# Moving the shared expert's second half product by a unit, with other banks and GpSimd for the first weight splits

## The chip, the cores and the metric

The kernel runs on one core of a Trainium2 chip. The metric is the device time of one execution in microseconds (us). Without the change it is 989.12 us, the median of three runs (989.07 to 989.73).

## The reference, cut to what matters

Sixteen sequences of 100 tokens with 512 features go through gated cross attention on 361 context keys each, and then through a feed-forward part with eight routed experts and one shared expert:

```python
x = x + tanh(g_xattn[0]) * xattn(layernorm(x), ctx_2048, Wq, Wk, Wv)   # 32 heads of 16, RMS-normed q and k
x = x + tanh(g_ffn[0]) * ffn(layernorm(x), router_w, w_gate_up, w_down, shared_gate_up, shared_down)
# ffn: router logits -> best expert e and gate = sigmoid(logit)
#   routed = silu(g) * u @ w_down[e],  (g, u) = (h * gate) @ w_gate_up[e]
#   shared = silu(g) * u @ shared_down, (g, u) = h @ shared_gate_up
#   return routed + shared
```

## The kernel before, in words

All engines run orders written out by hand in numbered **slots**. The loop over slots (L394 for TensorE, L528 for ScalarE, L690 for VectorE, L938 for GpSimd, L1333 for the DMA queue of SyncE) goes to slot 389; each engine does in slot s what is listed for s, in order, and semaphores make it wait. Sequence b is scored in slots 24b to 24b+23 as six **units** of four slots each: z = 0, 1 is the half of the heads, t = 0, 1, 2 the tile of keys. Unit n of sequence b is written (b, n) here, n = 3z + t.

For one unit TensorE makes scores (pe_scores, L490, into banks 4 to 7), ScalarE takes exp of them (act_exp, L663), and TensorE multiplies the probabilities with the values (pe_weighted_values, L505, called PV here, into bank 1). The next unit's scores wait for this unit's exp. Behind PV of n = 2 and n = 5 ScalarE takes bank 1 (act_take_outputs, L679 or L681) and so frees it for the next PV. For b < 15 a DMA transpose (L1314), a GpSimd copy (pool_join, L911), two small VectorE operations (dve_invert, L880 and L883) and two of GpSimd (pool_finish, L919 and L921) then bring the outputs back to x_all. For b = 15, TensorE turns them (pe_turn_outputs, L517, into bank 0) and VectorE finishes (dve_finish_last, L892 to L898).

Beside the scoring of b, sequence b+1 is prepared: projections (L472), sums of squares (L837), an inverse root in ten dependent steps on VectorE (dve_rms, L847 and then L769, L771, L773, L774), scaling (dve_scale, L859), packing into a high and a low f16 part (ScalarE L656, VectorE L866) and a transposing DMA each for the three key tiles and the queries (sp_turn_pack, L1307). Scores of unit (15, 0) wait for that of the queries (qT), whose issue in turn waits until q, key tile 0 and key tile 1 are all packed. In the last sequence ScalarE's packing of key tile 2 stands ahead of the exp of (15, 0) in its order. Nothing is projected beside the scoring of sequence 15, as there is no sequence 16.

The first piece of the feed-forward part is put into this thin stretch. The first weights of the shared expert are split into high and low parts in four pieces of 128 x 512: ScalarE writes high (act_first_high, L1409, slots 347, 348, 353, 354) and VectorE low = weight - high (dve_first_low, L1415, slots 348, 349, 356, 357). Pieces 0 and 1 are gate and up for the product's half j = 0, pieces 2 and 3 for j = 1. TensorE multiplies j = 0 in slots 351 (gate, bank 3) and 355 (up, bank 2), twelve matmuls each; VectorE copies both out (dve_first_copy, L1421). The half j = 1 comes in four **quarters** of six matmuls (pe_gate_up, L1475, slots 365, 369, 373, 377) into the same banks 3 and 2. In slot 386 the gate product of the next chunk follows. Then pe_shared begins, whose line of routing transposes (L1026) goes to banks 2 and 3 in turn, the first only when VectorE has multiplied (dve_mult, L1547) both halves of iteration 0. The slots of the last sequence on TensorE, as they run: 359 scores (15, 0); 363 scores (15, 1); 364 PV 0; 365 quarter; 367 scores 2; 368 PV 1; 369 quarter; 371 scores 3; 372 PV 2; 373 quarter; 374 turn of the outputs z = 0; 375 scores 4; 376 PV 3; 377 quarter; 379 scores 5; 380 PV 4; 384 PV 5; 386 next product; 387 turn of z = 1.

turn_order and wait_turn_bank (L365 and L432) keep the users of bank 0 in order, and product_bank (L1443) gives the bank of each gate and up product.

Of the kernel before, what the change touches and what calls it, by code (L numbers as in the profile page):

```python
# [20 lines left out]
F32 = mybir.dt.float32  # L21
# [18 lines left out]
HD = 16  # L40
# [38 lines left out]
FIRST_LOW_SLOTS = (348, 349, 356, 357)  # L79
FIRST_PRODUCT_SLOTS = (351, 355)  # L80
FIRST_COPY_SLOTS = (361, 362)
SECOND_PRODUCT_SLOTS = (365, 369, 373, 377)
NEXT_PRODUCT_SLOT = 386

DOWN_SLOT = 381
# [253 lines left out]
    return 24 * (b - 2) + LEAD  # L339


LAST_OUT_SLOTS = (14, 27)


def scoring(k, s):
    return [(b, s - 24 * b) for b in range(k.B) if 0 <= s - 24 * b < 40]
# [18 lines left out]
def turn_order(k):  # L365

    order = []
    for s in range(k.first_slot, k.last_slot):
        for b, j in preparing(k, s):
            order += [("src", b)] if j == SRC_SLOTS[2] else []  # L370
        for b, i in scoring(k, s):
            order += [("out", b, z) for z in range(2) if b == k.B - 1 and i == LAST_OUT_SLOTS[z]]
        for c, o in route_offsets(s):
            order += [("route", c, i) for i, at in enumerate((*ROUTE_TURN, ROUTE_LOGITS, ROUTE_BACK, ROUTE_RANK))
                      if o == at]
    return order, {name: n for n, name in enumerate(order)}
# [52 lines left out]
    return w  # L429


def wait_turn_bank(k, w, name):  # L432
    place = k.turn_place[name]
    if place:
        kind, *at = k.turn_names[place - 1]
        if kind == "src":
            w.wait_ge(k.src_low, 4 * at[0] + 3)
        elif kind == "out":
            w.wait_ge(k.finish_v, 2 * at[1] + 2)
        else:  # L440
            wait_route_taken(k, w, *at)


def pe_turn_source(k, PE, w, b):
    w.wait_ge(k.ident32_made, 2)
    w.wait_ge(k.xn_made, b + 1)
    wait_turn_bank(k, w, ("src", b))
    bank = k.bank[0]
    for j in range(k.KD):
        turned = PE.transpose(bank[:, P * j:P * j + k.N], k.xn[:, P * j:P * j + P], k.ident32[0:k.N, 0:k.N])  # L450
    turned.then_inc(k.src_turned, 1)
# [59 lines left out]

def pe_turn_outputs(k, PE, w, b, z):
    w.wait_ge(k.outs_taken, 2 * b + z + 1)
    wait_turn_bank(k, w, ("out", b, z))
    bank = k.bank[0]
    for j in range(4):
        turned = PE.transpose(bank[0:k.N, P * j:P * j + P], last_outs(k, z)[:, j, :], k.ident32[:])  # L517
    turned.then_inc(k.last_out_turned, 1)
# [5 lines left out]
def act_attention(k):  # L524
    A, w = k.A, Waits(k.A)
    for i, g in enumerate((k.g_xattn, k.g_ffn)):
        A.dma_start(k.gates[:, i:i + 1], g.rearrange("(a n) -> a n", a=1).to_broadcast([P, 1])).then_inc(k.gates_in, 16)
    for s in range(k.first_slot, k.last_slot):  # L528
        for n in (n for n, at in enumerate(WEIGHT_SLOTS) if prep_start(0) + at == s):
            act_weight_high(k, A, w, n)  # L530
        if s == prep_start(0) + 16:
            w.wait_ge(k.constants_made, k.n_constants)
        if unit_at(k, s):
            act_exp(k, A, w, s)
        for b, j in preparing(k, s):
            for p in range(4):
                if j == SRC_SLOTS[p] + 1:
                    act_source_high(k, A, w, b, TILE[p])
        if s == prep_start(0) + 16:
            w.wait_ge(k.gates_in, 32)  # L540
            A.activation(k.gates[:], k.gates[:], ACT.Tanh).then_inc(k.gates_ready, 1)
        for b, j in preparing(k, s):
            for n in range(7):
                if j == taken_slot(n):
                    if n in VALUE_AT:
                        act_copy_values(k, A, w, b, PROJECTION_TILE[n])
                    else:
                        act_take_heads(k, A, w, b, PROJECTION_TILE[n])
            for t in range(4):
                if j == PACK_SLOTS[t] + 1:  # L550
                    act_pack_high(k, A, w, b, t)
        for b, i in scoring(k, s):
            for z in range(2):
                if i == pv_slot(k, b, 3 * z + 2) + 1:
                    act_take_outputs(k, A, w, b, z)
        if s == ROUTER_SLOT:
            w.wait_ge(k.router_in, 16)
            A.activation(k.wrT[0][:], k.w_router_raw[:], ACT.Copy).then_inc(k.router_high, 1)
        for c, o in route_offsets(s):
            for j in range(CT):  # L560
                if o == ROUTE_TURN[j] + 1:
                    act_route_high(k, A, w, c, j)
            if o == ROUTE_LOGITS + 1:
                act_route_logits(k, A, w, c)
            if o == ROUTE_BACK + 2:
                act_route_gate(k, A, w, c)
        for n in range(4):
            if s == FIRST_SLOTS[n]:
                act_first_high(k, A, w, n)
        if s == DOWN_SLOT:  # L570
            act_part_high(k, k.first, A, w, 2)
    return w
# [114 lines left out]
def dve_attention(k):  # L687
    V, w = k.V, Waits(k.V)
    V.memset(k.bank[1][:, 0:GH * k.N], 0.0).then_inc(k.outs_cleared, 1)
    for s in range(k.first_slot, k.last_slot):  # L690
# [42 lines left out]
        for c, o in route_offsets(s):  # L733
# [12 lines left out]
                dve_route_place(k, V, w, c)  # L746
            if o == ROUTE_RANK + 2:
                dve_route_slot(k, V, w, c)
        for n in range(4):
            if s == FIRST_LOW_SLOTS[n]:  # L750
                dve_first_low(k, V, w, n)
        for which in range(2):
            if s == FIRST_COPY_SLOTS[which]:
                dve_first_copy(k, V, w, which)
# [131 lines left out]
def dve_finish_last(k, V, w, b, z):  # L886

    x, _, o = finish_views(k, b, z)
    turned = k.bank[0][0:k.N, :].rearrange("n (h c) -> n h c", c=2 * HD)
    w.wait_ge(k.x1_made, 2 * b + z)  # L890
    w.wait_ge(k.last_out_turned, z + 1)
    V.reciprocal(k.inv_sum[:], turned[:, :, HD]).then_inc(k.finish_v, 1)  # L892
    w.wait_ge(k.finish_v, 2 * z + 1)
    V.tensor_tensor(o, turned[:, :, 0:HD], k.inv_sum[:].unsqueeze(2).to_broadcast([k.N, 16, HD]),
                    MULT).then_inc(k.finish_v, 1)
    w.wait_ge(k.gates_ready, 1)
    w.wait_ge(k.finish_v, 2 * z + 2)
    V.scalar_tensor_tensor(out=x, in0=o, scalar=k.gates[0:k.N, 0:1], in1=x, op0=MULT, op1=ADD).then_inc(k.x1_made, 1)  # L898
# [25 lines left out]
def pool_attention(k):  # L924
# [13 lines left out]
    for s in range(k.first_slot, k.last_slot):  # L938
        for b, i in scoring(k, s):
            for z in range(2):  # L940
                if b + 1 < k.B and i == OUT_JOIN_SLOTS[z]:
                    pool_join(k, G, w, b, z)
                if b + 1 < k.B and i == OUT_JOIN_SLOTS[z] + 3:
                    pool_finish(k, G, w, b, z)
        for c, o in route_offsets(s):
            for j in range(CT):
                if o == ROUTE_GATED[j]:
                    pool_store_gated(k, G, w, c, j)
            if o == ROUTE_RELOAD:
                pool_reload(k, G, w, c)  # L950
        if s == FIRST_LOAD_SLOT:
            w.wait_ge(k.src_low, 4 * k.B)
            w.wait_ge(k.src_turned, k.B)
            for t in k.rows[2:4]:
                G.memset(t[:], 0.0).then_inc(k.rows_cleared, 1)
    return w


# [13 lines left out]
def wait_route_bank(k, w, c, i):  # L972

    place = route_place(c, i)
    if c < EARLY:
        wait_turn_bank(k, w, ("route", c, i))
    elif place < 4:
        w.wait_ge((k.first.mult, k.first.silu)[place % 2], 2)
    else:
        c_, i_ = divmod(place - 4, 7)  # L980
        wait_route_taken(k, w, c_ + EARLY, i_)
# [427 lines left out]
    A.activation(high, src, ACT.Copy).then_inc(k.first_high if n < 2 else k.first.w_high, 1)  # L1409


def dve_first_low(k, V, w, n):
    src, high, low = first_views(k, n)
    w.wait_ge(k.first_high if n < 2 else k.first.w_high, n % 2 + 1)
    V.tensor_tensor(low, src, high.bitcast(F32), SUB).then_inc(k.first_low if n < 2 else k.first.w_low, 1)  # L1415


def dve_first_copy(k, V, w, which):
# [14 lines left out]
def dve_part_low(k, r, V, w, part):  # L1433
    u, which = divmod(part, 3)
    high, low = k.w_split[u % 3][which]
    w.wait_ge(r.w_high, part + 1)
    V.tensor_tensor(low[:], k.w_raw[part % 4][:], high[:].bitcast(F32), SUB).then_inc(r.w_low, 1)  # L1437


# [3 lines left out]
def product_bank(r, it, j, which):  # L1443


    if it >= r.it0:
        return 2 * j + which
    return (3 - which, 4 + 2 * j + which, which)[min(it, 2)]


def pe_gate_up(k, r, PE, w, it, u, j, which, xs, width, share=0, shares=1):
# [8 lines left out]
    if r.it0 and it == 0:  # L1460
        if j == 0:
            w.wait_ge((k.v_copied, k.squared)[which], (k.NMT, k.NMT + 1)[which] * k.B)
        else:
            w.wait_ge(k.first_copied, which + 1)
    elif r.it0 and it == 1:
        w.wait_ge(k.exped, 6 * k.B)
    elif it <= r.it0:
        if r.it0 and it == 2:
            w.wait_ge(k.finish_v, 4)
        w.wait_ge(taken, 2 * it + (j if it < r.it0 else 0))  # L1470
    else:
        w.wait_ge(taken, 2 * it + j - 1)
# [613 lines left out]
```

## Time and profile before

| | value |
|---|---|
| median of three runs | 989.12 us |
| the profiled execution's own time | 988.57 us |
| its span | 986.6 us |
| TensorE busy in the span | 957.0 us, 97% |
| VectorE, ScalarE, GpSimd busy | 672.4, 559.2 and 161.7 us |
| mean granted TensorE clock | 0.997 |
| TensorE waits longer than noise from 550 us on | none |

Times in the rows count from the start of the span. In the page, PE is TensorE's matmuls, PEld its weight loads, DVE VectorE, ACT ScalarE, POOL GpSimd, SPq the DMA queue of SyncE. Between the profiled execution's time and its span lie 1.97 us of start and end.

### The profile page before, as it was taken

The page shows a single profiled execution, that of the slowest core. Times are in us where ns is not written, and L with a number is a line of the kernel's source. Part 1 is how long each engine was busy: PE and PEld are TensorE (multiplying, and loading weights), DVE is VectorE, ACT ScalarE, POOL GpSimd, SP SyncE. Part 2 cuts the span into 40 slices and gives each one's busy share as a digit, 9 for nine tenths or more (in the row PEclk, how much of TensorE's full clock was granted, in tenths as well). Part 3 has the DMA queues.
Part 4 walks back from the last instruction along what each step waited for, and adds up shares of the span by engine and source line. Part 5 has one row for each costly group of instructions (what it writes and reads, how often), then busy time and mean ns, then how long its engine had stood idle before and what let it go on. Part 6 is the DMA issues. An engine that isn't in the chain of part 4 may idle for free. (4 is left out here: it accounts for less than half of the span.)

```text
span 986.6 us, 25132 instructions
## 1 busy us (share of the span) xinstructions
PE 957.0 (97%) x10589; PEld 784.5 (80%) x10589; DVE 672.4 (68%) x1647; ACT 559.2 (57%) x851; POOL 161.7 (16%) x208
## 2 busy tenths in 40 slices
PE   5899999999999999999889999999999999999997
PEld 4677777777777777777777999999988988999886
DVE  6878886877658678687747534443477777777774
ACT  5576767777666777766752221222256666666663
POOL 2001111110112210112233300000110232012111
PEclk9999999999999999999999999999999999999999
DMA  7544344654337554346543401010377886787762
GB/s 263 142 92 84 78 91 105 122 90 88 80 73 169 110 100 83 71 91 150 128 101 107 114 22 43 22 43 21 123 239 224 243 244 215 220 244 240 224 197 69
DMA packets 176425, 127.38 MB, mean 129 GB/s; under 512 B 117246, under 2 KB 155134, under 8 KB 176308
## 3 DMA queue, kind: packets, MB, share of 16 engines
q1 hardware_dynamic: 166884, 105.98, 43.0%
q0 software_dynamic: 6544, 16.46, 5.4%
q10 hardware_dynamic: 2880, 3.29, 1.0%
q8 instruction: 85, 1.39, 0.6%
q14 instruction: 32, 0.26, 0.1%
HBM read 85.52 MB, written 13.56 MB: 100 GB/s over the span
## 5 line engine op out<-in xcount | busy, mean ns | idle before, releaser
L472 PE MATMUL bank<-arena_f32r 128*128 128x512 f32 (+2 forms) x1344 | 334.8, 400 | 11.4 <-DVE arena_f32r L823 10.1
L472 PEld LDWEIGHTS bank<-arena_f32r 128*128 128x128 f32 (+2 forms) x1344 | 234.8, 180 | 78.5 <-DVE arena_f32r L780 10.6
L663 ACT ACTIVATE probs<-score_banks 128x1600 f32<-128x1600 f32 x96 | 144.6, 1506 | 58.1 <-PE score_banks L490 58.0
L1536 ACT ACTIVATE hT_hi<-arena_f 128x224 fp32r<-128x224 f32 (+2 forms) x96 | 42.3, 441 | 116.7 <-DVE arena_f L1547 111.3
L1475 PE MATMUL bank<-xnT,arena_f32r 128*128 128x224 f32 (+1 forms) x720 | 103.2, 295 | 0.0
L1475 PEld LDWEIGHTS bank<-xnT,arena_f32r 128*128 128x128 f32 x720 | 97.7, 191 | 1.9 <-issue 0.8
L505 PEld LDWEIGHTS bank<-probs,values 128*17 128x17 f32 (+1 forms) x3072 | 62.7, 98 | 37.4 <-issue 22.3
L505 PE MATMUL bank<-probs,values 128*17 128x100 f32 (+1 forms) x3072 | 85.1, 252 | 3.2 <-ACT probs L663 2.5
L1547 DVE TENSOR_TENSOR arena_f<-bank,arena_f 128x224 f32<-128x224 f32 (+2 forms) x93 | 41.2, 443 | 65.6 <-PE bank L1475 65.1
L1437 DVE TENSOR_TENSOR arena_f32r<-arena_f,arena_f32r 128x1024 fp32r<-128x1024 f32 x43 | 52.7, 1226 | 19.2 <-ACT arena_f32r L1430 18.1
L911 POOL COPY heads_out<-outs 100x544 uint16<-100x544 uint16 x30 | 25.3, 843 | 203.6 <-DMA outs<-outT 202.8
L837 DVE TENSOR_REDUCE sumsq<-arena_f 128x32 f32<-128x512 f32 (+1 forms) x64 | 43.8, 685 | 21.5 <-ACT arena_f L625 21.4
L1562 PE MATMUL score_banks<-arena_f32r,hT_hi 128*128 128x512 f32 (+2 forms) x184 | 58.0, 396 | 0.0
L490 PE MATMUL score_banks<-qT,kT 32*128 32x100 f16 x3072 | 51.7, 205 | 5.5 <-ACT probs L663 3.0
L1493 PE MATMUL bank<-xnT,arena_f32r 128*128 128x448 f32 x168 | 55.8, 377 | 0.0
L1562 PE MATMUL score_banks<-wdown_lo,hT_hi 128*112 128x512 f32 (+2 forms) x140 | 55.1, 394 | 0.0
L1562 PE MATMUL score_banks<-wdown_hi,hT_hi 128*112 128x512 f32 (+2 forms) x140 | 55.1, 393 | 0.0
L490 PEld LDWEIGHTS score_banks<-qT,kT 32*128 32x128 f16 x3072 | 37.4, 93 | 20.9 <-issue 15.3
L1526 ACT ACTIVATE arena_f<-bank 128x384 f32<-128x384 f32 (+1 forms) x29 | 14.6, 505 | 64.9 <-PE bank L1475 64.7
L823 DVE TENSOR_TENSOR arena_f32r<-arena_f,arena_f32r 128x512 fp32r<-128x512 f32 (+1 forms) x48 | 31.9, 665 | 27.8 <-ACT arena_f32r L608 27.5
L1430 ACT ACTIVATE arena_f32r<-arena_f 128x1024 fp32r<-128x1024 f32 x43 | 45.1, 1048 | 8.4 <-DVE x_all L1720 8.4
L1720 DVE SCALAR_TENSOR_TENSOR x_all<-score_banks,gates,x_all 128x512 f32<-128x512 f32 (+1 forms) x52 | 38.6, 748 | 14.1 <-PE score_banks L1562 13.8
(275 smaller groups left out, 1850.8 us busy)
## 6 DMA issues: line engine op xcount, KB each, us to landing
arena_f<-L_ffn_w_gate_up SPq DMA_DIRECT2D x48, 512.0 KB
arena_f<-L_ffn_w_down SPq DMA_DIRECT2D x24, 512.0 KB
arena_f<-ctx SPq DMA_DIRECT2D x15, 722.0 KB, 4.2
w_raw<-L_ffn_w_gate_up SPq DMA_DIRECT2D x16, 512.0 KB
w_raw<-L_ffn_w_down SPq DMA_DIRECT2D x8, 512.0 KB
x_rows<-x_all SPq DMA_DIRECT2D x4, 800.0 KB
x_all<-x_rows POOLq DMA_DIRECT2D x4, 768.0 KB, 5.7
arena_f<-L_ffn_shared_gate_up SPq DMA_DIRECT2D x6, 512.0 KB
```

The lines of the kernel that those rows point to most:

```text
L472: product = PE.matmul(bank[0:rows, :], k.srcT[PLACE[t] % 2][a][:, j, 0:rows], weight, start=(m == 0), stop=(m == 11))
L490: product = PE.matmul(k.score_banks[:, j, k.N * r:k.N * r + k.N], k.kT[b % 2][rows, block, P * t:P * t + P], k.qT[b % 2][rows, part, block ...
L505: product = PE.matmul(k.bank[1][HW * j:HW * j + HD + 1, k.N * r:k.N * r + k.N], k.values[b % 2][0:m, t, 16 * z + GH * r + j, :], k.probs[n ...
L663: A.activation(k.probs[n % 2][:], k.score_banks[:, :, 0:GH * k.N].rearrange("p j (r n) -> p j r n", r=GH), ACT.Exp, scale=float(HD) ** -0. ...
L837: V.tensor_reduce(k.sumsq[b % 2][0:rows, t, :], k.square[0:rows, :].rearrange("p (h d) -> p h d", d=HD), AX.X, ADD).then_inc(k.summed, 1)
L1430: A.activation(k.w_split[u % 3][which][0][:], k.w_raw[part % 4][:], ACT.Copy).then_inc(r.w_high, 1)
L1437: V.tensor_tensor(low[:], k.w_raw[part % 4][:], high[:].bitcast(F32), SUB).then_inc(r.w_low, 1)
L1475: made = PE.matmul(bank[:, 0:width], weight[a][:, i, :], xs[x][:, i, 0:width], start=(i == 0 and n == 0), stop=(i == k.KD - 1 and n == 2))
L1493: PE.matmul(bank[:, 0:2 * SLOTS].rearrange("p (x n) -> p x n", x=2), high[:, i, :], xs[:, :, i, 0:SLOTS], start=(i == 0), stop=False)
L1536: A.activation(k.hT[it % 2][0][:, j, 0:width], k.hidden[j][:, 0:width], ACT.Copy).then_inc(r.h_high, 1)
L1547: V.tensor_tensor(h, up[:, 0:width], h, MULT).then_inc(r.mult, 1)
L1562: made = PE.matmul(bank[0:rows, :], k.hT[it % 2][h][:, j, r0:r0 + rows], weight[a][:, j, :], start=(first and j == 0 and n == 0), stop=(la ...
```

## The change

It has four parts. The quarters move to slots 361, 366, 370 and 373, and the two gate quarters go into bank 0 instead of bank 3, waiting for bank 0's last user in place of the copy of bank 3. The low parts of the four first weight pieces are made by GpSimd, at the end of the same slots, in place of VectorE. ScalarE takes the outputs of (14, z = 1) in slot 360, behind the exp of (15, 0), instead of slot 359 ahead of it. The last sequence's outputs are turned in bank 3 instead of bank 0, and later waits on the banks are changed to suit.

```diff
-SECOND_PRODUCT_SLOTS = (365, 369, 373, 377)
+SECOND_PRODUCT_SLOTS = (361, 366, 370, 373)
...
-LAST_OUT_SLOTS = (14, 27)
+LAST_OUT_SLOTS, LAST_OUT_BANK = (14, 27), 3
...
-        for b, i in scoring(k, s):
-            order += [("out", b, z) for z in range(2) if b == k.B - 1 and i == LAST_OUT_SLOTS[z]]
...
-def wait_turn_bank(k, w, name):
-    place = k.turn_place[name]
+def wait_turn_bank(k, w, place):
...
-        elif kind == "out":
-            w.wait_ge(k.finish_v, 2 * at[1] + 2)
...
     w.wait_ge(k.outs_taken, 2 * b + z + 1)
-    wait_turn_bank(k, w, ("out", b, z))
-    bank = k.bank[0]
+    w.wait_ge(*((k.finish_v, 2) if z else (k.first_copied, 1)))
+    bank = k.bank[LAST_OUT_BANK]
...
-                if i == pv_slot(k, b, 3 * z + 2) + 1:
+                if i == pv_slot(k, b, 3 * z + 2) + (2 if (b, z) == (k.B - 2, 1) else 1):
                     act_take_outputs(k, A, w, b, z)
...
-        for n in range(4):
-            if s == FIRST_LOW_SLOTS[n]:
-                dve_first_low(k, V, w, n)
...
-    turned = k.bank[0][0:k.N, :].rearrange("n (h c) -> n h c", c=2 * HD)
+    turned = k.bank[LAST_OUT_BANK][0:k.N, :].rearrange("n (h c) -> n h c", c=2 * HD)
...
+        for n in range(4):
+            if s == FIRST_LOW_SLOTS[n]:
+                pool_first_low(k, G, w, n)
...
-        w.wait_ge((k.first.mult, k.first.silu)[place % 2], 2)
+        w.wait_ge(*((k.finish_v, 4) if place % 2 else (k.first.mult, 2)))
...
-def dve_first_low(k, V, w, n):
+def pool_first_low(k, G, w, n):
     src, high, low = first_views(k, n)
     w.wait_ge(k.first_high if n < 2 else k.first.w_high, n % 2 + 1)
-    V.tensor_tensor(low, src, high.bitcast(F32), SUB).then_inc(k.first_low if n < 2 else k.first.w_low, 1)
+    G.tensor_tensor(low, src, high.bitcast(F32), SUB).then_inc(k.first_low if n < 2 else k.first.w_low, 1)
...
     w.wait_ge(r.w_high, part + 1)
+    w.wait_ge(r.w_low, 2 if r.u0 and part == 2 else 0)
...
-    return (3 - which, 4 + 2 * j + which, which)[min(it, 2)]
+    return (0 if (j, which) == (1, 0) else 3 - which, 4 + 2 * j + which, which)[min(it, 2)]
...
+        elif which == 0:
+            wait_turn_bank(k, w, len(k.turn_names))
         else:
-            w.wait_ge(k.first_copied, which + 1)
+            w.wait_ge(k.first_copied, 2)
...
         if r.it0 and it == 2:
-            w.wait_ge(k.finish_v, 4)
+            w.wait_ge(k.outs_taken, 2 * k.B)
```

## Rows read from the trace of the kernel before

**Rows 1.** The page, busy time, and the granted clock in 40 slices

```profile
PE 957.0 (97%) x10589; PEld 784.5 (80%) x10589; DVE 672.4 (68%) x1647; ACT 559.2 (57%) x851; POOL 161.7 (16%) x208
PEclk9999999999999999999999999999999999999999
```

**Rows 2.** Timeline of TensorE's matmuls: start, duration, line, operation, count, idle before

```profile
476.39 0.33 PE L1475 MATMUL bank<-xnT,w_first_gate_lo 128*128 128x384 f32 x1
477.83 0.53 PE L490 MATMUL score_banks<-qT,kT 32*128 32x100 f16 x32 [1.11 <-ACT probs L663]
...
482.37 0.53 PE L490 MATMUL score_banks<-qT,kT 32*128 32x100 f16 x32 [0.20 <-DMA qT<-q_pack]
484.85 0.77 PE L490 MATMUL score_banks<-qT,kT 32*128 32x100 f16 x32 [1.94 <-ACT probs L663]
485.55 1.54 PE L505 MATMUL bank<-probs,values 128*17 128x100 f32 x32
487.01 1.94 PE L1475 MATMUL bank<-xnT,arena_f32r 128*128 128x384 f32 x6
...
490.16 1.34 PE L1475 MATMUL bank<-xnT,arena_f32r 128*128 128x384 f32 x6
...
493.97 0.64 PE L517 MATMUL bank<-ident,outT 128*100 128x128 f32 x4
...
499.60 0.88 PE L505 MATMUL bank<-probs,values 105*17 105x100 f32 x32 [0.80 <-ACT probs L663]
...
505.75 0.54 PE L1026 MATMUL bank<-ident,rows 100*128 100x100 f32 x4 [0.44 <-DVE arena_f L1547]
```

**Rows 3.** Busy time of each engine in stretches, with granted clock (PEclk) behind POOL

```profile
484.00:485.00 1.00, 0.15 (x15) 0.18 (x19) 0.43 (x1) 0.70 (x1) 0.40 (x1) 1.00 0.50 100
485.00:486.00 1.00, 1.00 (x44) 0.85 (x39) 0.53 (x3) 0.34 (x1) 0.40 (x1) 0.50 0.98 180
488.00:489.00 1.00, 1.00 (x17) 0.76 (x19) 0.69 (x1) 0.00 (x0) 0.47 (x1) 0.80 0.61 136
```

**Rows 4.** Timeline of ScalarE

```profile
473.19 0.65 ACT L1409 ACTIVATE w_first_up_hi<-arena_f 128x512 fp32r<-128x512 f32 x1
474.35 1.06 ACT L656 ACTIVATE q_pack<-arena_f 100x1024 f16<-100x1024 f32 x1 [0.51 <-DVE arena_f L859]
...
477.65 1.16 ACT L1409 ACTIVATE arena_f32r<-arena_f 128x512 fp32r<-128x512 f32 x2
...
481.95 0.63 ACT L656 ACTIVATE k_pack<-arena_f 105x512 f16<-105x512 f32 x1 [1.75 <-DVE arena_f L859]
482.49 0.82 ACT L679 ACTIVATE outT<-bank 128x800 uint16<-128x800 uint16 x1
483.20 1.50 ACT L663 ACTIVATE probs<-score_banks 128x1600 f32<-128x1600 f32 x1
485.65 1.51 ACT L663 ACTIVATE probs<-score_banks 128x1600 f32<-128x1600 f32 x1 [0.95 <-PE score_banks L490]
```

**Rows 5.** Timeline of VectorE

```profile
470.15 0.55 DVE L769 TENSOR_SCALAR rms<-sumsq 128x32 int32<-128x32 int32 x1
...
471.56 0.19 DVE L774 SCALAR_TENSOR_TENSOR rms<-rms_tmp,rms 128x32 f32<-128x32 f32 x1
...
473.03 0.68 DVE L1415 TENSOR_TENSOR w_first_gate_lo<-arena_f,w_first_gate_hi 128x512 fp32r<-128x512 f32 x1
473.63 0.68 DVE L859 TENSOR_TENSOR arena_f<-arena_f,rms 100x512 f32<-100x512 f32 x1
...
481.23 0.69 DVE L859 TENSOR_TENSOR arena_f<-arena_f,rms 105x512 f32<-105x512 f32 x1
```

**Rows 6.** Timeline of GpSimd

```profile
470.04 0.62 POOL L919 TENSOR_TENSOR heads_out<-heads_out,inv_sum 100x256 f32<-100x256 f32 x1 [5.08 <-DVE inv_sum L883]
470.74 0.74 POOL L921 TENSOR_TENSOR x_all<-x_all,heads_out 100x256 f32<-100x256 f32 x1
...
491.82 0.29 POOL L1740 CAST arena_f32r<-spill_hi 128x128 fp32r<-128x128 f32 x1
```

More of the change, by code:

```diff
@@ L446, in pe_turn_source @@
     w.wait_ge(k.xn_made, b + 1)
-    wait_turn_bank(k, w, ("src", b))
+    wait_turn_bank(k, w, k.turn_place["src", b])
     bank = k.bank[0]
@@ L975, in wait_route_bank @@
     if c < EARLY:
-        wait_turn_bank(k, w, ("route", c, i))
+        wait_turn_bank(k, w, k.turn_place["route", c, i])
     elif place < 4:
-        w.wait_ge((k.first.mult, k.first.silu)[place % 2], 2)
+        w.wait_ge(*((k.finish_v, 4) if place % 2 else (k.first.mult, 2)))
     else:
```

## The prediction

> **What bounds the kernel now.** I read the page first: TensorE is busy 97% of the span and its clock is full [rows 1], so only a stretch in which TensorE idles, or works at a lower clock, can give time back. Behind the attention part TensorE has no real waits, so a shift there reaches the end one for one. The change touches one stretch, sequence 15, and there the timeline of TensorE has what the averages hide [rows 2]: idle of 1.11 us before 477.83, of 1.94 us before the scores at 484.85, of 0.80 us before the last PV at 499.60. The windows show what comes of the longest [rows 3]: the granted clock is 1.00 to 485, 0.50 from 485 on, and 0.80 in the slice of 488, so full again at about 488.4. These are 2.4 and 1.2 GHz. In between PV takes 1.54 us and a quarter 1.94 us, against 0.88 us and 1.34 us later [rows 2]. Both stand ahead of the next scores, so the low clock costs 0.66 + 0.60 = 1.3 us, and some 0.2 us on the scores themselves.
>
> What ends the waits are two chains. One is exp to scores to exp: from the start of one exp to that of the next takes at least 1.5 for the exp and 0.5 for the scores with about half a us of handovers, some 2.5 us; 483.20 to 485.65 is one such step [rows 4]. The other leads into it: the scores of (15, 0) at 482.37 waited for the transposed queries [rows 2], and the exp at 483.20 stood behind the packing of key tile 2 and the taking of bank 1 [rows 4].
>
> **The change without a price for GpSimd.** VectorE drops four subtractions of 0.68 us, 0.60 from start to start. One (473.03) stands right before the scaling of q at 473.63 [rows 5], which ScalarE's packing of q waits for (idle 0.51 us) [rows 4]. So that chain could come 0.5 us earlier. A quarter goes into the idle time before 484.85, where it costs nothing as long as the exp of (15, 0) covers it (1.3 us under 1.94), and keeps TensorE busy there. Taking bank 1 moves from before the exp of (15, 0) (0.71 us from 482.49 to 483.20) to behind it; the next exp needs 0.5 us of scores first, so only some 0.1 to 0.2 us of it shows, and PV of (15, 0) starts about when that exp does. The moved turn, two additions of a wait on things done long before (bank 0's last user, the copies), and the later bank waits cost nothing: TensorE reaches each well after. The order on the queues stays, though the DMA that carries (14, 1) out leaves about 1.3 us later, hidden because only GpSimd and x_all's statistics need it. This all gives: exp of (15, 0) at 482.45, of (15, 1) at 484.7 to 485, and with steps of 2.7, 2.6, 3.1 (with the turn, 0.64) and 2.5 us the last PV at about 497.3 instead of 499.60, **2.3 us gained**.
>
> **The price of GpSimd.** The trace of before has no 128x512 subtraction on GpSimd. The nearest rows have 256 columns and take 0.62 and 0.74 us; a copy of 128 columns takes 0.29 us, which bounds the fixed part [rows 6]. From 2 x 0.62 - 0.29 = 0.95 to 2 x 0.74 = 1.48 us; I take 1.25 us, near twice their mean with a little fixed cost off. The Trainium skill (GPSIMD Engine Reference, Reconciling with measured numbers) gives 4497 ns for 2048 columns; that would make it about 1.1 us and move the sum by 0.3 us at most.
>
> The larger matter is that the two engines stand in each other's way. VectorE's step at 470.15 takes 0.55 us, where a like step takes 0.19 us [rows 5]: it is over at 470.70, when GpSimd's operation of 470.04 to 470.66 is [rows 6]. So it did nothing until about 470.51, 0.15 us before GpSimd's recorded end. A subtraction of 1.25 us then holds VectorE for about 1.05 us. The Trainium skill (SBUF - State Buffer, SBUF: two separate sides) has the rule for it: VectorE operations with two SBUF inputs or in a 2-port mode and those of GpSimd exclude each other for the whole instruction, and whichever starts first has its way. This trace agrees (0.55 against 0.19 us), and the rule speaks against this change: the steps of the inverse root are of this kind.
>
> Step by step, with these rows:
> - Piece 0 is ready at about 471.5, when GpSimd's previous operation ends (471.48). VectorE is in the middle of the root for q (step at 471.56), with seven steps of 0.225 us to go, which ended at 473.1. They are held once: end at about 474.05, +0.95 us.
> - Piece 1 is ready when ScalarE's high part ends, 473.19 + 0.65 = 473.84. GpSimd asks at about 473.9 and gets its turn between the last step and the scaling of q, which is held to 475.05: +1.05 us. VectorE no longer has its own subtraction before it: -0.60 us. The scaling ends 1.4 us later than before, at 475.7 for 474.3.
> - ScalarE packs q 1.4 us later, and all behind it in its order moves along, the exps of (14, 4) and (14, 5) and the high parts at 477.65 with them [rows 4]; the packing of key tile 1 and the qT transpose too. Scores of (15, 0): 482.37 + 1.4 = 483.8.
> - Pieces 2 and 3 are then at about 479.7 to 482.2, upon the root for key tile 2: held 1.05 + 0.85 us, less two subtractions of 0.60, on top of the 1.4 us. The scaling at 481.23 goes to 483.3, ScalarE's packing (0.6) ends at 484.6, and there the exp of (15, 0) starts, 483.20 before: +1.4. Then the taking, and the exp of (15, 1) at 486.8 (485.65 before).
> - From there by the work between: PV 0.81 and a quarter 1.31 and scores 0.46 from start to start, 2.6 to 2.7 us for two steps at full clock; 3.2 us with the turn; 2.2 us for the last, as the work is gone and only the exp chain counts; then 1.5 us of exp. 486.8 + 2.7 + 2.65 + 3.2 + 2.2 + 1.5 = 499.05, the last PV, against 499.60.
>
> Behind it (next product, turn, VectorE's finish, the routing transpose with its 0.44 us of waiting at 505.75 [rows 2]) everything follows as before. **Sum: -0.55 us**, 988.57 to 988.0 for the profiled execution. The median of the runs shown is 0.55 us above that execution, so 988.6; the roundings favour the change a little (a quarter less at half clock), and I say 988.5.
>
> **The rivals.**
> 1. *The piece misses the scaling.* Piece 1 and the scaling are within 0.1 us of each other (473.9 and 474.03). If the hold of piece 0 is 0.15 us shorter, the scaling goes first and GpSimd waits: q comes 0.4 us late instead of 1.4, the rest by a like amount: last PV at 498.1, 987.6 us. For it: the margin. Against it: at 470.15 VectorE was the one that waited, with a similar lead of GpSimd's.
> 2. *No price.* The subtractions fall into VectorE's gaps, or hold it much less than 1 us: 2.3 to 2.6 us gained, 986.7 us. The rows of 0.55 us speak against it; for it speaks that a later piece 0 or 1 would find VectorE with PSUM work only.
> 3. *Slower: the clock falls in the idle time that grows.* By the steps above TensorE idles from 476.7 [rows 2] to 479.2, 2.5 us, where it was 1.11; before, 1.94 us of idle came before the fall of 485 [rows 3]. Over 3.3 us at 1.2 GHz the up product (12 matmuls) takes up to 2 x 0.60 = 1.2 us more and pushes PV and the scores of (15, 0) by 0.9 to 1.0 us: 989.5 us. It decides from 0.55 us on, which is all the gain there is. Against it: 1.9 us of dense matmuls stand just ahead of the gap, where the gap of 484.85 had 1.6 us of light ones and a scores step. With the upper price of GpSimd (1.48) 0.3 us more, 989.8.
> 4. *The clock falls late.* In slots 375 to 384 no quarter is left; TensorE idles 0.8 us before the scores of (15, 5) and 0.9 before the last PV. If the clock fell there, the 24 matmuls behind would cost 1.6 us: 990.1. The single gap of 0.80 before 499.60 did not do it.
>
> **How the numbers follow.** A difference of 0.2% (2.0 us) is about what a measurement of this kernel tells from none: faster is below 987.1, slower above 991.1. Chances: the sum with held VectorE 0.40; rival 1 0.17; rival 2 0.20; rival 3 0.13; rival 4 0.06; anything else 0.04, half of it slow. Rival 2 whole and the lower part of rival 1 are faster: 0.25. Slower by 2.0 us needs rivals 3 and 4 together or a price outside the bounds: 0.07. The rest, 0.68, is within. The range goes from 986.5 (all of rival 2) to 990.1 (rival 4).
>
> **What would show it.** In the changed profile: (a) subtractions on GpSimd of about 1.25 us, at 471.5, 473.9, and two near 480; (b) a step of the root for q at about 471.8 of 1.2 us instead of 0.19, and a scaling of q that ends near 475.7 (rival 1: 474.7; rival 2: 473.8); (c) scores of (15, 0) at 483.8 (482.8; 481.9); (d) full clock from 484 to 490, quarters of 1.3 us and PV of 0.9 us, and no other slice at 0.50 (rivals 3 and 4: one from 479 or 498 on); (e) the last PV near 499.0. I am wrong if the scaling of q is not held, if the clock falls elsewhere, or if TensorE waits in slots 361 to 366 for bank 0 or for piece 2.

## The result, and the profile after

| | before | after |
|---|---|---|
| median of 14 runs each | 988.98 us | 992.00 us |
| lowest and highest | 986.14, 989.88 | 988.22, 995.43 |
| ratio after to before, 95% interval | | 1.0030 (1.0018 to 1.0041) |
| the profiled execution's own time, span | 988.57, 986.6 | 994.18, 992.2 |
| a second profile of each kernel (e10, e8): own time, span | 988.33, 986.4 | 990.22, 988.2 |

The changed kernel is slower by about 3 us in these runs, and by 1.8 us in a second set of ten (990.63 against 988.86, ratio 1.0020, 1.0010 to 1.0031). I had forecast 988.5 and a range up to 990.1. Two slow executions, 5261 us of before and 1551 us of e7, are in no figure of this document.

Of the 5.6 us between the first two spans, 3.6 us are not the change's: the exp of (14, 3), the last landmark ahead of the moved work, starts at 471.33 before and at 474.96 after. Of these, 2.0 us come in at 44 us, where the clock fell once in this execution, 1.1 us before that point and 0.5 us near 130 us. Over the twelve other profiles of this study, of kernels that do the same work up to there, that exp starts anywhere from 470.55 to 473.48. So from here on I count from it; the table holds the stretch.

| from the start of the exp of (14, 3), us | before | again (e10) | after | again (e8) |
|---|---|---|---|---|
| scaling of q ends | 2.98 | 2.97 | 4.64 | 4.64 |
| scaling of key tile 2 ends | 10.59 | 10.58 | 13.15 | 13.14 |
| exp of (15, 0) starts | 11.87 | 11.87 | 14.54 | 14.54 |
| exp of (15, 1) starts | 14.32 | 14.09 | 16.78 | 16.77 |
| last PV starts | 28.27 | 26.95 | 29.96 | 29.66 |
| end of the span | 515.27 | 513.99 | 517.24 | 516.75 |

The timeline of VectorE after (start, duration, line, operation) and, under it, that of GpSimd show what holds the root. They answer to [rows 5] and [rows 6]:

```profile
474.36 0.19 DVE L765 SCALAR_TENSOR_TENSOR rms_tmp<-rms 128x32 f32<-128x32 f32 x1
474.58 0.57 DVE L767 TENSOR_TENSOR rms_tmp<-rms_tmp,sumsq 128x32 f32<-128x32 f32 x1
475.19 1.30 DVE L768 SCALAR_TENSOR_TENSOR rms<-rms_tmp,rms 128x32 f32<-128x32 f32 x1
476.52 0.19 DVE L765 SCALAR_TENSOR_TENSOR rms_tmp<-rms 128x32 f32<-128x32 f32 x1
...
477.65 1.22 DVE L768 SCALAR_TENSOR_TENSOR rms<-rms_tmp,rms 128x32 f32<-128x32 f32 x1
478.91 0.69 DVE L853 TENSOR_TENSOR arena_f<-arena_f,rms 100x512 f32<-100x512 f32 x1
...
483.84 1.17 DVE L768 SCALAR_TENSOR_TENSOR rms<-rms_tmp,rms 128x32 f32<-128x32 f32 x1
485.05 1.21 DVE L765 SCALAR_TENSOR_TENSOR rms_tmp<-rms 128x32 f32<-128x32 f32 x1
...
487.42 0.69 DVE L853 TENSOR_TENSOR arena_f<-arena_f,rms 105x512 f32<-105x512 f32 x1
```

```profile
475.14 1.30 POOL L1412 TENSOR_TENSOR w_first_gate_lo<-arena_f,w_first_gate_hi 128x512 fp32r<-128x512 f32 x1
477.54 1.28 POOL L1412 TENSOR_TENSOR w_first_up_lo<-arena_f,w_first_up_hi 128x512 fp32r<-128x512 f32 x1 [1.10 <-ACT w_first_up_hi L1406]
483.65 2.55 POOL L1412 TENSOR_TENSOR arena_f32r<-arena_f,arena_f32r 128x512 fp32r<-128x512 f32 x2 [4.83 <-ACT arena_f32r L1406]
```

Each of the four subtractions (1.28 to 1.30 us) has a step of the root beside it that takes 1.17 to 1.30 us instead of 0.19. The timeline of ScalarE carries it on; it waits 2.17 us for q and 2.65 us for key tile 2, 0.51 and 1.75 us before [rows 4]. The exp of (15, 0) then stands 0.73 us more, and not for key tile 2: it waits for its scores.

```profile
479.63 1.06 ACT L653 ACTIVATE q_pack<-arena_f 100x1024 f16<-100x1024 f32 x1 [2.17 <-DVE arena_f L853]
...
488.14 0.63 ACT L653 ACTIVATE k_pack<-arena_f 105x512 f16<-105x512 f32 x1 [2.65 <-DVE arena_f L853]
489.50 1.51 ACT L660 ACTIVATE probs<-score_banks 128x1600 f32<-128x1600 f32 x1 [0.73 <-PE score_banks L487]
```

TensorE's matmuls (columns as in [rows 2]) show the idle time that grew, a slow product and slow PVs, and a wait of 0.94 us within the scores of (15, 4) that was 0.20 us before:

```profile
483.11 0.53 PE L487 MATMUL score_banks<-qT,kT 32*128 32x100 f16 x32 [2.77 <-ACT probs L660]
...
485.72 0.84 PE L1475 MATMUL bank<-xnT,w_first_up_hi 128*128 128x384 f32 x2
486.36 0.52 PE L1475 MATMUL bank<-xnT,w_first_up_lo 128*128 128x384 f32 x1
486.81 2.17 PE L502 MATMUL bank<-probs,values 128*17 128x100 f32 x64
488.92 0.53 PE L487 MATMUL score_banks<-qT,kT 32*128 32x100 f16 x32
...
491.15 0.54 PE L487 MATMUL score_banks<-qT,kT 32*128 32x100 f16 x32 [0.46 <-ACT probs L660]
491.79 0.88 PE L502 MATMUL bank<-probs,values 128*17 128x100 f32 x32
492.60 1.34 PE L1475 MATMUL bank<-xnT,arena_f32r 128*128 128x384 f32 x6
...
500.88 0.30 PE L487 MATMUL score_banks<-qT,kT 32*128 32x100 f16 x9 [0.94 <-issue]
...
504.92 0.88 PE L502 MATMUL bank<-probs,values 105*17 105x100 f32 x32 [0.80 <-ACT probs L660]
```

That wait in the timeline of before:

```profile
495.23 0.22 PE L490 MATMUL score_banks<-qT,kT 32*128 32x100 f16 x4 [0.20 <-issue]
```

In the changed kernel the scores of (15, 0), at 488.92, start at the end of the slow PV of 486.81, with no idle time between. So q's delay reached the exp of (15, 0) through TensorE: later exps of (14, 4) and (14, 5), a longer gap before the scores of (14, 5) at 483.11, and the low clock behind it.

And the windows, with the granted clock behind POOL's busy time as in [rows 3]:

```profile
484.00:485.00 1.00, 1.00 (x7) 1.00 (x6) 1.00 (x1) 1.00 (x2) 1.00 (x2) 0.85 0.81 148
485.00:486.00 1.00, 1.00 (x4) 1.00 (x4) 0.97 (x2) 0.50 (x1) 1.00 (x1) 0.50 1.74 150
488.00:489.00 1.00, 1.00 (x51) 0.84 (x44) 0.30 (x2) 0.63 (x1) 0.00 (x0) 0.94 1.10 209
```

The fall behind the exp of (15, 0) is gone (that exp starts at 489.50 here), but the clock falls earlier in the program, behind the idle time of 2.77 us. What I set as full clock from (15, 0) on is there: the wait ahead of the scores of (15, 1) is 0.46 us instead of 1.94, quarters take 1.3 and PVs 0.9 us.

### The profile page after: what moved, and what is told of

Its sections match the earlier page's. It is cut to its first block and busy times, and to the rows that moved or that the text cites. A ratio compares the mean times of both kernels' runs of the same rounds, so it can differ in the third digit from the quotient of the medians.

```text
span 992.2 us, 25132 instructions
## 1 busy us (share of the span) xinstructions
PE 958.9 (97%) x10589; PEld 785.7 (79%) x10589; DVE 674.4 (68%) x1643; ACT 560.1 (56%) x851; POOL 165.9 (17%) x212
## 3 DMA queue, kind: packets, MB, share of 16 engines
q8 instruction: 85, 1.39, 0.6%
## 5 line engine op out<-in xcount | busy, mean ns | idle before, releaser
L653 ACT ACTIVATE k_pack<-arena_f 128x512 f16<-128x512 f32 (+1 forms) x48 | 30.3, 632 | 31.7 <-DVE arena_f L853 31.7
```

## The experiments

Two theories stood against each other. **H**: GpSimd's subtractions hold VectorE, and that is the loss; the rest of the change gains. **R**: the moved quarters, the bank or the later taking cost the time. All landmarks are counted from the exp of (14, 3).

**e1 and e9: all but GpSimd.** The changed kernel with the subtractions back on VectorE; e9 is the same kernel once more.

```diff
-                pool_first_low(k, G, w, n)
+                dve_first_low(k, V, w, n)      # in dve_attention, ahead of dve_first_copy, as before
```

> The change with its four subtractions back on VectorE; all else as changed. Theory H (GpSimd's subtractions hold VectorE's root for q and key tile 2, and the wait that this makes lets TensorE's clock fall): the scaling of q ends as before (2.7 us after the start of the exp before it, the one of (14, 3), not 4.6), there is no slice at 0.50 near the up product, and the time is 1.5 to 2.5 us below the kernel before. Theory R (the moved quarters, the bank or the later taking of bank 1 cost the time): as slow as the changed kernel, about 3 us above before.

> The kernel of e1_rest_only once more: its profile had the last PV at 25.94, 2.3 us earlier than before, its times only 0.5 us less. If the stretch's gain is real in every run and the first timing was scatter: the same landmarks to 0.1 us, and a median 1.5 to 2.5 us below before. If something ahead of the stretch gives it back: the same landmarks and again within 1 us of before.

Measured: scaling of q at 2.99 in both, last PV at 25.94 and 25.91, no slice at a lower clock around it. TensorE in e1:

```profile
483.43 0.53 PE L487 MATMUL score_banks<-qT,kT 32*128 32x100 f16 x32 [0.20 <-DMA qT<-q_pack]
483.89 1.32 PE L1481 MATMUL bank<-xnT,arena_f32r 128*128 128x384 f32 x6
485.67 0.54 PE L487 MATMUL score_banks<-qT,kT 32*128 32x100 f16 x32 [0.45 <-ACT probs L660]
...
498.33 0.88 PE L502 MATMUL bank<-probs,values 105*17 105x100 f32 x32 [0.80 <-ACT probs L660]
```

The quarter sits in the former gap. H holds and R falls: the last PV comes 2.33 us before that of the first profile. The sum without a price for GpSimd had 2.3, but in part by luck: it had the exp of (15, 0) at 11.12 from the landmark, 0.75 us earlier than before, and e1 has it at 11.62 (it keeps the subtractions on VectorE, and the exp waits 0.38 us for its scores); from there to the last PV it had 14.85 us, and e1 took 14.32. The times say less: medians 988.54 (11 runs) and 987.81 (12 runs) beside 989.02 and 989.33 of before, both ratios 0.9994 (0.9983 to 1.0005; 0.9982 to 1.0006). The mean of the 23 is 988.4 against 989.1 for 102 runs of before (91 measured beside the variants and the 11 of e10), 0.7 us with a standard error of 0.35. That is less than the stretch gives, and less than the 1.5 to 2.5 us that I expected; e10 shows one reason.

**e10: before again.**

> The kernel before, unchanged, for a second profile. The scaling of q at 2.98, the last PV at 28.27 with a fall of the clock behind the exp of (15, 0); where there is no such fall (the mean clock of a few runs is 0.999), about 27. Ratio to before 1.000, within 0.001.

The ratio is 0.9998 (0.9987 to 1.0009), and the profile is of an execution in which the clock did not fall, though TensorE idled just as long:

```profile
485.92 0.54 PE L490 MATMUL score_banks<-qT,kT 32*128 32x100 f16 x32 [1.95 <-ACT probs L663]
486.39 0.88 PE L505 MATMUL bank<-probs,values 128*17 128x100 f32 x32
487.20 1.34 PE L1475 MATMUL bank<-xnT,arena_f32r 128*128 128x384 f32 x6
```

Its last PV is at 26.95, 1.3 us before that of the first profile. So the fall is worth 1.3 us and does not come in every run, and by these profiles the rest of the change is worth 1.0 us in a run without it and 2.3 us in one with it. That explains only part of what the times lack. Searched over its whole span, a profile has a mean clock of 0.999 or 1.0 where the clock never fell, 0.997 or 0.998 with one fall and 0.995 with two (falls in the last 4 us aside). Only 15 of the 102 runs of before are at 0.999 or more (mean 987.9 us), so most have a fall; of the 23 of e1 and e9 it is 14 (mean 987.55). Within this group the two differ by 0.3 us, with a standard error of 0.5. The rest of the shortfall is open.

**e2: GpSimd alone.** The kernel before with only the subtractions moved (the same lines as in the change).

> The kernel before with only the four subtractions moved to GpSimd. Theory H: the scaling of q ends 1.6 us later than before, the exp of (15, 0) starts 2 to 3 us later; as the idle time ahead of the scores of (15, 1) stays too, 2 to 4 us slower than before. Theory R: within 0.5 us of before.

Measured: median 991.59 us (7 runs), ratio 1.0021 (1.0006 to 1.0036); scaling of q at 4.63, key tile 2 at 13.14, exp of (15, 0) at 14.67, last PV at 30.26, 2.0 us behind before. This part by itself makes the loss. The clock falls here too, just before the grown gap ends (0.81 in the slice of 480, scores at 480.91), and no second time in the old one (1.98 us idle, at 489.1):

```profile
481.00:482.00 1.00, 1.00 (x33) 0.85 (x34) 0.90 (x4) 1.00 (x3) 0.55 (x1) 0.50 0.01 1
```

**e11, e7, e3 and e12: which piece.** The changed kernel with only some pieces on GpSimd: piece 0 (e11), 0 and 1 (e7), 2 and 3 (e3, and e12 once more).

```diff
-            if s == FIRST_LOW_SLOTS[n]:
+            if s == FIRST_LOW_SLOTS[n] and n in (0,):         # e11; (0, 1) in e7; (2, 3) in e3 and e12
                 pool_first_low(k, G, w, n)
```

> The changed kernel with only piece 0 on GpSimd, the other three on VectorE (one more semaphore, so that each has its own). Theory H: one step of q's root takes 1.2 to 1.3 us, the other not, and the scaling of q ends at 3.5 to 3.6 (2.98 with none, 4.64 with two): the two holds add up as 0.5 + 1.1. The exp of (14, 4) at 5.5. If a single hold is absorbed: 3.0.

> The changed kernel with pieces 0 and 1 on GpSimd and pieces 2 and 3 on VectorE, the mirror of e3. If the two holds of q's root do the harm: scaling of q ends at 4.64 as in the changed kernel, TensorE idles 2.8 us before the scores of (14, 5) and the clock can fall; key tile 2's scaling ends near 12.2; last PV at 28.5 to 29.7. If the four holds add up evenly: last PV at 27.9.

> The changed kernel with pieces 0 and 1 on VectorE and only pieces 2 and 3 on GpSimd. Theory H: q is on time, key tile 2's root is still held twice (its scaling 0.5 to 1 us later than before), TensorE's gap before the scores of (14, 5) is 1.1 us again and the clock does not fall there: 0.5 to 2 us faster than before. If the clock falls for another reason: 1 to 3 us slower.

> The kernel of e3_gpsimd_last_two once more (last PV at 26.38, median 987.79 of 11 runs, the lowest so far). By its landmarks it should be 0.2 to 0.4 us behind e9_rest_only_again and 1.5 to 2 us below before; if it comes out below e9 by more than 0.5 us again, something outside the stretch decides.

| | scaling of q | key tile 2 | exp of (15, 0) | last PV | median (runs) |
|---|---|---|---|---|---|
| none (e1) | 2.99 | 10.58 | 11.62 | 25.94 | 988.54 (11) |
| piece 0 (e11) | 3.61 | 11.21 | 13.52 | 28.67 | 989.37 (10) |
| 0 and 1 (e7) | 4.64 | 12.25 | 13.28 | 29.20 | 989.45 (9) |
| 2 and 3 (e3) | 2.98 | 11.51 | 12.08 | 26.38 | 987.79 (11) |
| 2 and 3 (e12) | 2.98 | 11.50 | 12.07 | 28.31 | 988.81 (12) |
| all (after) | 4.64 | 13.15 | 14.54 | 29.96 | 992.00 (14) |

The holds add up as the steps said: piece 0 moves q by 0.62, piece 1 by another 1.03, pieces 2 and 3 key tile 2 by 0.9. In e11 one step of the root is held and the other is not:

```profile
472.69 1.30 DVE L771 SCALAR_TENSOR_TENSOR rms<-rms_tmp,rms 128x32 f32<-128x32 f32 x1
474.02 0.19 DVE L768 SCALAR_TENSOR_TENSOR rms_tmp<-rms 128x32 f32<-128x32 f32 x1
...
475.15 0.19 DVE L771 SCALAR_TENSOR_TENSOR rms<-rms_tmp,rms 128x32 f32<-128x32 f32 x1
475.38 0.69 DVE L856 TENSOR_TENSOR arena_f<-arena_f,rms 100x512 f32<-100x512 f32 x1
```

What comes later differs between executions. In e11 the clock fell behind the gap, which is 1.74 us there (0.50 in the slice of 481), and took the exp of (15, 0) 0.24 us past that of e7, where it did not fall, although e7's q is a microsecond later. e3 and e12 are one kernel, and 1.9 us apart in the last PV. In e12 TensorE waits for the transposed key tile 2, which e3 does not:

```profile
490.75 0.53 PE L487 MATMUL score_banks<-qT,kT 32*128 32x100 f16 x32 [1.28 <-DMA kT<-k_pack]
```

That DMA was issued at 12.92 and 12.93 in the two; in e12 it let the scores go at 17.77, in e3 they went at 16.43 without a wait. Before, it was issued at 12.0. What differs beside it is the next transposing DMA on the same queue, the one of the outputs of (14, 1): in e12 it was issued 1.39 us behind (487.29 after 485.90) and key tile 2 landed after 4.8 us, in e3 2.91 us behind and key tile 2 landed after 3.0 us.

```profile
485.90 1.23 SPq L1307 DMA_TRANSPOSE kT<-k_pack  x1
487.29 1.33 SPq L1314 DMA_TRANSPOSE outs<-outT  x1
```

e5, below, is the only other profile with so close a pair (1.40 us) and so late a landing (4.9 us); in the remaining eleven the pair is 2.1 us or more apart and key tile 2 lands after 3.0 to 3.8 us. No run set this distance on purpose, so that the one makes the other is not shown.

**e5: the changed kernel without the fall.** Twelve matmuls whose result is not used, in the idle time ahead of the scores of (14, 5).

```diff
+        if s == FIRST_PRODUCT_SLOTS[0]:
+            for n in range(12):
+                PE.matmul(k.bank[0][:, 0:k.width[0]], k.w_first[0][0][:, n % 4, :],
+                          k.xnT[0][0][:, n % 4, 0:k.width[0]], start=True, stop=True)
```

> The changed kernel with twelve more matmuls (about 2.1 us, into bank 0, never read) behind the first gate product, in the 2.8 us in which TensorE waits for the exp of (14, 4). Counted from the start of the exp of (14, 3). If the fall of the clock is a cost of its own: no slice at 0.50 near the up product, PV of (14, 4) and (14, 5) takes 1.6 us instead of 2.17, the exp of (15, 0) starts about 1 us earlier than the changed kernel's 14.54, limited by key tile 2 (scaling still at 13.1), so at about 13.8, and the last PV at 29.0 to 29.4 instead of 29.96. If the fall is hidden behind the held VectorE: 29.96 stays within 0.2.

```profile
481.32 0.53 PE L491 MATMUL score_banks<-qT,kT 32*128 32x100 f16 x32 [0.64 <-ACT probs L664]
...
484.09 1.57 PE L506 MATMUL bank<-probs,values 128*17 128x100 f32 x64
...
492.65 0.53 PE L491 MATMUL score_banks<-qT,kT 32*128 32x100 f16 x32 [1.33 <-DMA kT<-k_pack]
```

The clock stays at 1.00, PV takes 1.57 instead of 2.17 us and the exp of (15, 0) starts at 13.74 instead of 14.54: the fall costs at least 0.80 us there (13.8 was expected; the exp now follows the packing of key tile 2 at once, so that is what ends last). But the last PV is at 30.14, not at 29.0 to 29.4: the saved time turned into the wait for the transposed key tile 2, which is issued as late as in the changed kernel (14.58 and 14.57) and lands later, and the median is 991.96 us (7 runs), ratio 1.0022. Keeping TensorE busy did not mend this.

**e6 and e4: which of the other parts gains.** e6 is e1 with the quarters in their old slots, e4 is e1 with the outputs of (14, z = 1) taken in slot 359.

```diff
-SECOND_PRODUCT_SLOTS = (361, 366, 370, 373)     # e6
+SECOND_PRODUCT_SLOTS = (365, 369, 373, 377)
...
-                if i == pv_slot(k, b, 3 * z + 2) + (2 if (b, z) == (k.B - 2, 1) else 1):     # e4
+                if i == pv_slot(k, b, 3 * z + 2) + 1:
```

> As e1_rest_only (subtractions on VectorE, new banks, later taking), but the quarters in their old slots. Theory: the quarters' slots carry the gain, by filling the idle time ahead of the scores of (15, 1), which also kept the clock from falling. Then the clock falls to 0.50 again around the second to fifth microsecond behind the exp of (15, 0), quarter and PV slow down, and the last PV is at 27.5 to 28.3, close to the 28.27 of before. If the later taking carries it: about 26.

> As e1_rest_only, but ScalarE takes the outputs of (14, z = 1) ahead of the exp of (15, 0), as before. If the later taking is worth what I gave it (0.7 us off the path to that exp, 0.1 to 0.2 us back at the next): 0.3 to 0.7 us slower than e1_rest_only. If another wait ends last there (the transposed queries): the same as e1_rest_only within 0.2 us.

e6: last PV at 28.51 (25.94 in e1), median 988.86 (10 runs), ratio 1.0001 (0.9991 to 1.0011). TensorE waits 1.70 us again and the clock falls:

```profile
484.00:485.00 1.00, 1.00 (x44) 0.85 (x39) 0.33 (x2) 0.68 (x2) 0.61 (x1) 0.50 1.11 206
```

The slots carry the gain: 2.57 us between the two profiles, of which 0.69 us is a wait within the scores of (15, 4), described below, that e1 has not. e4: exp of (15, 0) at 11.87 instead of 11.62, last PV at 26.01 instead of 25.94, median 988.63. The later taking wins 0.25 us at the exps of (15, 0) and (15, 1) and gives most of it back by that of (15, 2) (16.64 against 16.58); I had put 0.3 to 0.7 us on it.

**e8: the changed kernel again**, its landmarks are in the first table.

> The changed kernel unchanged, for a second profile. The order of the work is fixed, so the same holds (scaling of q at 4.64, key tile 2 at 13.15) should stand in it to 0.05 us. Where the clock falls may differ: a fall behind the 2.8 us of idle time in most runs, and none, or one more in the late gaps, in some. Time 989 to 995 us with a mean near 992.

The holds are equal to 0.01 us, and the clock falls in the same product (0.59 in the slice of 481, 0.50 in that of 482). The mean of its ten runs is 990.8 us, below the 992 expected; with the first fourteen it is 991.5 us, 2.3 us above the 989.1 of before. The stretch is 1.4 to 1.7 us longer in the two profiles than in the first of before, and 2.7 to 3.0 us longer than in e10.

## Why the prediction was wrong

In one sentence: the sum put the clock's fall in the grown idle time and the late wait within the scores of (15, 4) at nothing and took the holds too small, and these cost 0.8, 0.9 and 0.5 us in the first profile.

**Right:** the first half of the mechanism of the likeliest case. GpSimd and VectorE exclude each other, the steps of the root are held, and q and then key tile 2 are late. The other half was not as written: the sum lets the packing of key tile 2 release the exp of (15, 0), and in both profiles of the changed kernel that exp waited 0.72 to 0.73 us more for its scores. Only with TensorE at full clock (e5) did key tile 2 end last. The Trainium skill has a rule for the exclusion (SBUF - State Buffer, SBUF: two separate sides), and this trace agrees with it: 1.17 to 1.30 us for a step of 0.19 us in four places out of four. Also right was that the low clock's share of the gain without GpSimd is 1.3 us (e10). That the sum of that gain came out (2.3 us forecast, 2.33 in e1) is partly luck, as said with e1. Rival 1, that piece 1 misses the scaling, did not occur: 0.1 us of margin was enough in every profile with that piece on GpSimd, though it caught the root's last step and not the scaling.

**Wrong, by steps:**
1. *The forecast chose no fall of the clock.* Rival 3 had it, in the right place and for the right reason: the idle time from 476.7 to 479.2 was forecast as 2.5 us, measured 2.77, and the clock fell in the product behind it in both profiles of the changed kernel. e5 gives its price at the exp of (15, 0) as 0.80 us; I had said 0.9 to 1.0. I gave the rival 0.13 because of the dense matmuls ahead of the gap. They did not prevent it: of the four profiles with this gap (after, e8, e2, e7) three have the fall.
2. *The holds were a little undersized, all in one direction.* Subtractions of 1.28 instead of 1.25 us held 1.0 to 1.1 us each: q late by 1.66 for 1.4, key tile 2 late by 2.56 for 2.1 us. With step 1 the exp of (15, 0) is 2.67 us late where I had 1.4, and that of (15, 1) 2.46 for 1.15. These two are the main part of the error: 1.3 us, 0.8 of it the fall and 0.5 the holds.
3. *The way from the exp of (15, 1) to the last PV* was forecast as 12.25 us and took 13.18 and 12.89 us; in e1 it took 12.08. The difference is mostly the wait within the scores of (15, 4), which the profile puts down to issue (the engine waited for nothing that it shows): 0.20 and 0.26 us before, 0.94 and 0.62 after, 0.42 to 0.93 in e2, e5, e6, e7, e11 and e12, none in e1, e3, e4 and e9. I had no term for it. The DMA view has more: in all ten profiles with the wait it ends 2.3 to 2.6 us behind a packet on the queue q8, which the profile calls instruction (after: packet at 23.4, matmuls on at 25.92). In the four without it that packet comes 3.1 to 3.7 us ahead of these scores (e1: 18.6, scores at 21.66). So it looks like a wait for instructions that were fetched late. No run tested that, and what makes the packet late is open.
4. *The base of the sum.* It was made against an execution with a fall worth 1.3 us and counted its removal as a gain of every run. e10 has none. This alone makes the gain without GpSimd 1.0 us in such a run, but by the mean clocks only 15 of 102 runs of before are of that kind.

Landmark by landmark the sum in the first profile is +1.69 us at the last PV instead of -0.55: 1.3 us from steps 1 and 2, 0.9 us from step 3. That leaves the medians. The first fourteen runs of the changed kernel are 3.0 us above before, more than the first profile's 1.7 us at the last PV and 2.0 us at the end. Their mean granted clock goes from 0.992 to 0.999, and the time goes with it: 994.9 us at 0.992, 991.3 at 0.997, 989.7 at 0.999. Seven of them are at 0.995 or lower, against 8 of 102 runs of before. So in some executions the clock falls more than once. This goes with pieces 0 and 1 on GpSimd: 12 of 47 runs of the kernels that have both there (after, e8, e2, e5, e7) are at 0.995 or lower, 11 of 179 of all others. But it is uneven, as none of e8's ten runs of the same kernel is. Where the further falls are, no profile shows: the first profile of after has one fall at 44 us besides, and e4, e5 and e12 have it too, so that one is not the change's.

**The range** ended at 990.1 because it took rivals 3 and 4 one at a time and left the late wait of step 3, and the transposed key tile 2 of e5 and e12, out.

The best version is the change without its GpSimd part, 988.4 us in the mean of 23 runs, or with pieces 2 and 3 on GpSimd, 988.5 us in the mean of 23. Both are 0.7 us below before, too little to call it faster. In the profiles the former is 0.4 to 2.4 us ahead of the latter.

## What to carry to other kernels

- An elementwise operation moved to an idle GpSimd was not free for VectorE here: price it as its own length, less some 0.2 us, added to the chain of small dependent VectorE steps that it lands in, and look for a row in which both engines already overlap. Of four pieces the two beside the critical root did the harm, the two later ones cost 0.4 us at the last PV where nothing else came in the way (e3), and 2.4 us where a DMA did (e12).
- When a step makes a chain later, follow the delay to the idle time of TensorE that it makes, and ask there for the clock. Then ask which of the late chains ends last, as the delay may arrive through TensorE and not through the engine that was held. And count a gain from a fall that goes away only as often as the fall comes: look at the mean clock of all runs, not at the profiled one.
- Profiles of a kernel whose runs scatter by some 2 us are best compared from a landmark ahead of the change.

## What the runs showed of the hardware that was not expected

- The same idle time of 1.94 and 1.95 us of one kernel was followed by a fall to 1.2 GHz in one execution and by none in another, at a difference of 1.3 us. The idle time of 2.76 to 2.77 us behind 2.3 us of dense matmuls was followed by a fall in three of four profiles (after, e8, e2, not e7), one of 1.74 us at that place too (e11); with the time cut to 0.64 us (e5) there was none. So the length of the gap alone does not tell, and falls came behind gaps of 1.70 (e6) and 1.74 us.
- GpSimd's 128x512 f32 subtraction took 1.28 to 1.30 us, 1.9 times VectorE's 0.68 us, and held VectorE for about 1.0 to 1.1 us of it.
- A transposing DMA that was issued at the same point (12.93 and 12.92) let TensorE go by 16.43 in one execution and only at 17.77 in another; it landed after 3.0 and 4.8 us. Over fourteen profiles the two late landings (4.8 and 4.9 us) are those with another transposing DMA issued 1.4 us behind.
- A run of 32 small score matmuls was broken by a wait of 0.20 to 0.94 us in ten of fourteen profiles, each time ending 2.3 to 2.6 us behind a packet of 0.02 MB on the instruction queue.
